# The four compute engines' slots 16 to 79 and SP's layers 1 to 4 of both transformer stacks: unrolled code becomes a loop

## The chip, the cores and the metric

One core of a Trainium2 chip runs the whole program in one launch. The metric is the device time of the program in microseconds; lower is better. A core has five engines, each with its own instruction stream: TensorE (PE), VectorE (DVE), ScalarE (ACT), GpSimd (POOL) and SyncE (SP, which here issues all DMA copies inside the stacks). They meet only through semaphores.

## The reference

A hybrid block over x of 4 sequences x 512 tokens x 128 (float32), four parts, each on the layer norm of x and added to x:

```python
x = x + _L0_attn_a_ref(_layernorm(x), ...)   # retention
x = x + _L0_ffn_ref(_layernorm(x), ...)      # stack 0: six layers
x = x + _L0_attn_b_ref(_layernorm(x), ...)   # a scan over time
x = x + _L0_ffn_ref(_layernorm(x), ...)      # stack 1: the same six layers again
```

The change touches only the two calls of the stack, which is:

```python
def attn_layer(x, Wqkv, qs, ksc, Wo):        # 16 heads of 64, window 32
    q, k, v = split(x @ Wqkv)
    q = l2norm(q) * qs;  k = l2norm(k) * ksc
    q = q * cos * scale + rotate_half(q) * sin * scale
    k = k * cos / scale + rotate_half(k) * sin / scale
    # each window of 32 queries sees its own 32 keys and the 32 before, masked
    return softmax(q @ k.T * 8) @ v @ Wo
def ffn_layer(x, g, bln, W1, b1, W2, b2):
    a, gate = split((layernorm(x) * g + bln) @ W1 + b1)
    return a * gelu(gate) @ W2 + b2
for i in range(6):
    x = attn_layer(shift_tokens(x), ...) + x
    x = ffn_layer(shift_tokens(x), ...) + x
```

## The kernel before

`program` (L2448) runs retention, stack 0, the mixer (the scan) and stack 1; each phase is a block that all engines enter and leave together. Both stacks come out of `ffn_stack` (L348).

**Tiles, groups, slots.** A tile is 128 tokens; a group is the 4 tiles of one sequence in one layer; a stack has 6 layers x 4 sequences = 24 groups = 96 tiles (`TILES`). The work is a software pipeline written out by hand. In slot N an engine works on parts of several tiles at once: the projections of tile N-4, the turning (transposes) of tile N-5 or N-6, the scores of N-6, the softmax of N-7 and N-8, the weighing of the values of N-9, the output projection of N-10, and the MLP of group G-3 or G-4. What a slot holds, and in which order, depends only on its place in the group, T = N % 4. Each of the four compute engines has its own `slot(N, T, G, at, of)` with that order as four branches (PE L719, ACT L985, DVE L1210, POOL L1370). `at(lag)` gives the tile that lies `lag` slots back, `of(lag)` its group. There are 112 slots per stack: 96 and 16 to fill and drain the pipeline; `live` and `live_group` drop the parts of tiles that don't exist.

**`slots` and `run_slots`** (L476, L480) call the slot's body. `run_slots(tile, group, layer, odd, slots_run)` writes `slots_run` slots from tile number `tile` on. In the kernel before there is one call, `run_slots(0, 0, 0, 0, TILES + 16)`, with plain integers: all 112 slots stand in each engine's stream as straight code, with every semaphore value, tile row and address a constant.

**Order between engines.** Every finished step increments a semaphore of its own (`done[...]`); `wait` (L445) and `wait_group` (L451) compare it with tile or group number plus a constant. Beside the data's own waits PE has many that only set its order (L720 to L860). Each engine's instructions run in the order written. Eight PSUM banks: four work banks handed round by the table `BANK`, two for scores (`bank_s`), two for the weighed values (`bank_o`).

**`apart`** (L464) adds 1 to a semaphore that nobody reads, `passed`, and only where the number that it is given is not a plain int. In the kernel before it thus emits nothing. It stands behind the waits of `scores` (L618), `weigh` (L635), the first projection of a group (L602), `mask_max` (L1114), and behind each of SP's waits in `spread_values`, `spread_probs` and `layer_loads`.

**PE** makes each fp32 product as two matmuls with two weight loads in the trace: a projection (`project`, L597) is 128x512, `scores` (L618) is 128 matmuls of 64x64 per tile with no wait inside, `weigh` (L635) 128 of 64x32.

**DVE** does, per tile, four rotations of two instructions (`rotate`, L1065, L1077 and L1079, which read the tables `rot[:, g.layer, T]`), four sums of squares (L1088), the four small steps of the inverse norm (`norms`, L1091), two masks with row maximum (`mask_max`, L1114, 8 pairs of a custom instruction and a read of its accumulator each), two sums and reciprocals, two transposes of the probabilities (L1148), and the residual (`mid`). **ACT** squares, copies out of PSUM and exponentiates; **POOL** adds the rotated halves (L1334), scales them (L1344), and subtracts the maximum and scales in the softmax (L1352, L1360).

**SP** (L495) issues, for each tile, four copies that spread the values to other partitions (`spread_values`, L510) and eight for the probabilities (`spread_probs`, L526), each set behind three waits, and in the first eight tiles of a layer two pieces of the next layer's `w_qkv`, at tile 4 `w_o`, at tile 11 the MLP's weights (`layer_loads`, L544). Weights are double-buffered by layer (`half`). `layer_loads` is called with layer 0, 1, 2, 3, 4, 5 as plain integers.

The code is in none of its parts a loop on the chip.

## Time and profile before

| | us |
|---|---|
| median of 3 runs | 3611.79 |
| lowest, highest | 3595.09, 3617.66 |
| profiled execution, device time | 3617.66 |
| profiled execution, span from first to last instruction | 3615.8 |
| mean granted clock of PE, share of full | 0.967 |
| stack 0, first projection to last weighing | 105.8 to 1607 |
| mixer | about 1640 to 2060 |
| stack 1, first projection to last weighing | 2074.3 to 3580 |

The profile is of one execution. Its page lists each engine's busy time, its slices, the DMA queues, and groups of instructions. "Idle before" is an engine's idle time ahead of an instruction, with what ended it; "issue" there is idle time that ended through nothing the profile shows. PEld is PE's weight load, which overlaps PE. DMA-issuing instructions of SP are listed under SPq. Ends of matmuls are modelled. The queues named "instruction" carry the engines' own code.

### The profile page before, as it was taken

The numbers are of one execution on the slowest core, as the hardware profiler recorded it, in microseconds if no ns is written. First come the engines' busy times: TensorE is split into PE (matmuls) and PEld (weight loads), VectorE is DVE, ScalarE is ACT, GpSimd is POOL, SyncE is SP. The second block draws the span as 40 slices with busy tenths as digits, with TensorE's granted clock in tenths as the row PEclk, the third lists the DMA queues.
The fourth block names the chain that finished last, engine by engine and source line by source line (L and its number), as shares of the span: only waits on it lengthen the run. The fifth ranks groups of instructions, "written<-read, shape, count | busy, mean of one in ns | idle before, by whom it ended". The sixth has DMA issues, their size and how long they took to land. (4 is left out here: it accounts for less than half of the span.)

```text
span 3615.8 us, 151302 instructions
## 1 busy us (share of the span) xinstructions
PE 3373.0 (93%) x60144; PEld 2187.3 (60%) x60144; DVE 3356.0 (93%) x11899; ACT 2045.9 (57%) x3659; POOL 2704.3 (75%) x2440
## 2 busy tenths in 40 slices
PE   6799999999999999988699689999999999999997
PEld 4366666666666666653466446666666666666664
DVE  6899999999999999965799799999999999999994
ACT  2456666665665666654422146666666566666663
POOL 1788888888888888843144288888888888888882
PEclk9899999999999999998799689999999999999999
DMA  1233333333333333320000123333333333333322
GB/s 44 60 88 82 76 91 75 91 78 81 92 76 77 87 81 71 73 66 17 0 1 1 36 49 90 79 89 80 72 93 80 78 90 79 76 92 72 75 67 66
DMA packets 151806, 250.42 MB, mean 69 GB/s; under 512 B 42688, under 2 KB 73408, under 8 KB 150976
## 3 DMA queue, kind: packets, MB, share of 16 engines
q1 hardware_dynamic: 151104, 240.75, 27.8%
q8 instruction: 479, 7.85, 1.0%
q14 instruction: 223, 1.83, 0.2%
HBM read 38.21 MB, written 1.05 MB: 11 GB/s over the span
## 5 line engine op out<-in xcount | busy, mean ns | idle before, releaser
L605 PE MATMUL stack_work<-stack_w_qkv,stack_xst 128*128 128x512 f32 x2304 | 1171.2, 615 | 20.0 <-ACT stack_sq L878 15.6
L1334 POOL TENSOR_TENSOR stack_roped<-stack_rot_c,stack_rot_s 128x512 f32<-128x512 f32 x768 | 973.4, 1280 | 231.7 <-DVE stack_rot_s L1079 120.6
L1344 POOL TENSOR_TENSOR stack_roped<-stack_roped,stack_rnorm 128x512 f32<-128x512 f32 x768 | 790.6, 1043 | 173.3 <-DVE stack_rnorm L1111 173.3
L878 ACT ACTIVATE stack_sq<-stack_work 128x512 f32<-128x512 f32 x768 | 457.2, 595 | 739.7 <-DVE stack_rot_s L1079 734.6
L605 PEld LDWEIGHTS stack_work<-stack_w_qkv,stack_xst 128*128 128x128 f32 x2304 | 388.0, 193 | 289.9 <-issue 219.4
L1077 DVE TENSOR_TENSOR stack_rot_c<-stack_work,rot_tables 128x512 f32<-128x512 f32 x768 | 516.2, 672 | 30.6 <-PE stack_work L605 26.9
L1079 DVE TENSOR_TENSOR stack_rot_s<-stack_work,rot_tables 128x512 f32<-128x512 f32 x768 | 518.7, 675 | 0.0
L1088 DVE TENSOR_REDUCE stack_ssq<-stack_sq 128x8 f32<-128x512 f32 x768 | 512.1, 672 | 3.3
L1122 DVE CUSTOM_DVE_ANT_0 stack_s_m<-stack_bank_s,band 128x64 f32<-128x64 f32 x3072 | 468.9, 215 | 17.7 <-PE stack_bank_s L629 12.8
L614 PEld LDWEIGHTS stack_work<-ident,stack_roped 128*128 128x128 f32 x3072 | 353.6, 141 | 168.9 <-issue 143.2
L614 PE MATMUL stack_work<-ident,stack_roped 128*128 128x128 f32 x3072 | 436.8, 278 | 19.8 <-ACT stack_sq L878 9.8
L1360 POOL TENSOR_TENSOR stack_s_m<-stack_s_m,stack_inv 128x512 f32<-128x512 f32 x384 | 417.0, 1086 | 32.1 <-DVE stack_inv L1140 32.1
L1352 POOL TENSOR_TENSOR stack_s_m<-stack_s_m,stack_smax 128x512 f32<-128x512 f32 x384 | 400.8, 1044 | 32.6 <-DVE stack_smax L1122 30.4
L652 PEld LDWEIGHTS stack_bank_o<-stack_p_pairs,stack_v_even 64*64 64x64 f32 x12288 | 330.0, 135 | 155.5 <-issue 155.3
L665 PEld LDWEIGHTS stack_work<-stack_o_t,stack_w_o 128*128 128x128 f32 x3072 | 364.1, 192 | 80.9 <-issue 58.6
L629 PEld LDWEIGHTS stack_bank_s<-stack_k_t,stack_q_t 64*32 64x32 f32 x24576 | 277.7, 105 | 189.5 <-issue 181.5
L652 PE MATMUL stack_bank_o<-stack_p_pairs,stack_v_even 64*64 64x32 f32 x12288 | 379.0, 221 | 10.3 <-issue 7.3
L652 PE MATMUL stack_bank_o<-stack_p_pairs,stack_v_nat 64*64 64x32 f32 x12288 | 376.7, 219 | 8.1 <-issue 8.0
L665 PE MATMUL stack_work<-stack_o_t,stack_w_o 128*128 128x128 f32 x3072 | 369.4, 276 | 5.0 <-issue 4.0
L629 PE MATMUL stack_bank_s<-stack_k_t,stack_q_t 64*32 64x64 f32 x24576 | 319.3, 225 | 32.8 <-issue 32.5
L652 PEld LDWEIGHTS stack_bank_o<-stack_p_pairs,stack_v_nat 64*64 64x64 f32 x12288 | 331.9, 135 | 9.9 <-issue 9.8
L904 ACT COPY stack_q_t<-stack_work 128x512 f32<-128x512 f32 x384 | 226.5, 590 | 157.5 <-PE stack_work L614 156.9
(255 smaller groups left out, 5110.6 us busy)
## 6 DMA issues: line engine op xcount, KB each, us to landing
stack_v_even<-stack_v_nat SPq DMA_DIRECT2D x768, 128.0 KB, 2.4
stack_p_pairs<-stack_p_turned SPq DMA_DIRECT2D x1536, 64.0 KB
stack_w_qkv<-table_ffn_qkv SPq DMA_DIRECT2D x192, 96.0 KB, 2.2
stack_w_o<-table_ffn_wo SPq DMA_DIRECT2D x12, 512.0 KB, 4.4
stack_w<-table_ffn_w SPq DMA_DIRECT2D x12, 384.0 KB
stack_w<-table_ffn_w SPq DMA_DIRECT2D x12, 192.0 KB
x_outer<-L_attn_a_X SPq DMA_DIRECT2D x4, 256.0 KB, 7.6
ret_xpos<-table_xpos SPq DMA_DIRECT2D x1, 1024.0 KB, 6.9
```

The source lines that it names most:

```text
L605: pe.matmul(work[(BANK["p_" + c][T] + g.row) % 4][:, :], xst[:, g.row, P * T:P * (T + 1)], w_qkv[:, g.half, col:col + 512], start=True, st ...
L614: last = pe.transpose(bank[:, P * n:P * (n + 1)], roped[:, CHUNKS.index(c), T % 2, P * n:P * (n + 1)], ident[:, :])
L629: last = pe.matmul(bank_s[j][WINDOW * n:WINDOW * (n + 1), 64 * hp:64 * hp + 64], q_t[rows, T % 2, hp, WINDOW * n:WINDOW * (n + 1)], k_t[ro ...
L652: last = pe.matmul(bank_o[HD * odd:HD * (odd + 1), two, at:at + WINDOW], values[:, 2 * m + j, :], p_pairs[rows, T % 2, odd_window, j, 2 * ...
L665: last = pe.matmul(bank[:, 0:P], w_o[:, g.half, n, :], o_t[:, T % 2, n, :], start=n == 0, stop=n == PAIRS - 1)
L878: act.activation(sq[:, i % 2, :], work[(BANK["p_" + c][T] + g.row) % 4][:, :], ACT.Square).then_inc(done["squared_" + c], 1)
L1077: dve.tensor_tensor(rot_c[:, i % 2, :].rearrange("p (h d) -> p h d", h=8), src.rearrange("p (h d) -> p h d", h=8), cosine, ALU.mult)
L1079: dve.tensor_tensor(rot_s[:, i % 2, :].rearrange("p (h f d) -> p h f d", h=8, f=2), src.rearrange("p (h f d) -> p h f d", h=8, f=2)[:, :, ...
L1088: dve.tensor_reduce(ssq[:, T % 2, i, :], sq[:, i % 2, :].rearrange("p (h d) -> p h d", h=8), AX.X, ALU.add).then_inc(done["summed_" + c], 1)
L1122: last = dve.tensor_tensor_reduce(s_m[:, T % 2, j, hp, :], bank_s[j][:, 64 * hp:64 * hp + 64], mask[:, first:first + 2 * WINDOW], 1.0, LOW ...
L1334: pool.tensor_tensor(roped[:, i, T % 2, :], rot_c[:, i % 2, :], rot_s[:, i % 2, :], ALU.add).then_inc(done["roped_" + c], 1)
L1344: pool.tensor_tensor(r, r, rnorm[:, T % 2, i, :].unsqueeze(2).broadcast_to([P, 8, HD]), ALU.mult).then_inc(done["united_" + c], 1)
```

## The change

Each compute engine's 112 slots are now emitted in three pieces: slots 0 to 15 as straight code; a loop `Fori(0, 2)` whose body holds 32 slots and runs twice, for slots 16 to 79; and slots 80 to 111 as straight code. The body covers two layers (32 tiles), so that the buffer halves stay constants (`odd` is 1), as do T, the bank, the rows of `xst`, `roped`, `q_t` and so on. Tile, group and layer numbers in it are a register times a constant plus a number; so each semaphore value in `wait`, `wait_group`, `wait_x` and the DMA waits is one, and so is the address `rot[:, g.layer, T]` in DVE's rotations. `live` is always true there, and `apart` emits its increment.

On SP `layer_loads` for layers 1 to 4 becomes one body in `Fori(1, 5)`. Its weight loads have addresses that depend on the layer's register (`w["qkv"][layer]`, and `layer % 2` for the half); the copies of values and probabilities keep constant addresses, and all its waits compare with register values, each followed by `apart`'s increment. Layers 0 and 5 stay straight.

No engine's work, order or buffer is changed. `Fori` is a loop on one engine alone: it adds to a register at the end of the body and branches back while the register is below the end; engines don't meet at it.

```diff
-            run_slots(0, 0, 0, 0, TILES + 16)
+            run_slots(0, 0, 0, 0, 16)
+            with eng.Fori(0, 2) as pair:
+                run_slots(32 * pair + 16, 8 * pair + 4, 2 * pair + 1, 1, 32)
+            run_slots(16 * (DEPTH - 1), 4 * (DEPTH - 1), DEPTH - 1, 1, 16 + 16)
@@ SP
-            for layer in range(1, DEPTH - 1):
+            with sp.Fori(1, DEPTH - 1) as layer:
                 layer_loads(layer, False, False)
```

## Rows read from the trace of the kernel before

**Rows 1.** The page: busy time of the engines, VectorE's 40 slices, an instruction queue
```profile
PE 3373.0 (93%) x60144; PEld 2187.3 (60%) x60144; DVE 3356.0 (93%) x11899; ACT 2045.9 (57%) x3659; POOL 2704.3 (75%) x2440
...
DVE  6899999999999999965799799999999999999994
...
q8 instruction: 479, 7.85, 1.0%
```

**Rows 2.** Windows: us, busy us of each engine (xinstructions), granted clock, DMA share, GB/s
```profile
300.00:600.00 300.00, 297.26 (x5970) 196.09 (x5969) 297.09 (x1142) 191.85 (x346) 259.19 (x237) 1.00 0.35 83
...
900.00:1200.00 300.00, 293.84 (x5823) 193.33 (x5821) 293.35 (x1119) 189.53 (x341) 255.45 (x233) 0.99 0.35 82
```

**Rows 3.** ScalarE's copy of the heads, L929, 150 to 600 us: ns min/median/max, starts
```profile
L929 ACT COPY stack_o_t<-stack_bank_o x29: 1017/1037/1072, 172.8 to 598.7; 128x1024 f32<-128x1024 f32 x29
```

**Rows 4.** Groups by line, 600 to 1100 us: xcount, busy us, mean ns, idle before, releasers
```profile
L1079 DVE TENSOR_TENSOR stack_rot_s<-stack_work,rot_tables 128x512 f32<-128x512 f32 x129 | 87.2, 676 | 0.0
L1077 DVE TENSOR_TENSOR stack_rot_c<-stack_work,rot_tables 128x512 f32<-128x512 f32 x129 | 86.8, 673 | 4.2 <-PE stack_work L605 3.5
...
L605 PEld LDWEIGHTS stack_work<-stack_w_qkv,stack_xst 128*128 128x128 f32 x385 | 64.6, 192 | 42.9 <-issue 33.2 <-ACT stack_sq L878 7.2
```

**Rows 5.** Timeline of TensorE near 861 us: start, us, line, xcount, idle before
```profile
860.64 1.32 PE L629 MATMUL stack_bank_s<-stack_k_t,stack_q_t 64*32 64x64 f32 x107
863.79 0.64 PE L629 MATMUL stack_bank_s<-stack_k_t,stack_q_t 64*32 64x64 f32 x21 [1.82 <-issue]
```

**Rows 6.** The window of 2 us behind that pause, columns as in rows 2
```profile
865.00:867.00 2.00, 2.00 (x3) 0.67 (x2) 1.32 (x11) 0.61 (x2) 2.00 (x3) 0.50 0.91 203
```

**Rows 7.** Timeline of VectorE behind that pause
```profile
869.54 0.59 DVE L1159 TENSOR_TENSOR stack_mshift<-stack_work,stack_xst 64x128 f32<-64x128 f32 x2 [3.22 <-PE stack_work L665]
```

**Rows 8.** Timeline: the first and the last engine to begin one slot
```profile
699.66 0.59 PE L605 MATMUL stack_work<-stack_w_qkv,stack_xst 128*128 128x512 f32 x1
...
701.85 1.28 POOL L1334 TENSOR_TENSOR stack_roped<-stack_rot_c,stack_rot_s 128x512 f32<-128x512 f32 x1 [0.23 <-DVE stack_rot_s L1079]
```

**Rows 9.** Timeline of VectorE, 703 to 715 us
```profile
703.03 0.68 DVE L1079 TENSOR_TENSOR stack_rot_s<-stack_work,rot_tables 128x512 f32<-128x512 f32 x1
...
703.63 0.70 DVE L1148 STREAM_TRANSPOSE stack_p_turned<-stack_s_m 128x512 f32<-128x512 f32 x1
...
709.43 0.21 DVE L1122 CUSTOM_DVE_ANT_0 stack_s_m<-stack_bank_s,band 128x64 f32<-128x64 f32 x1
...
709.57 0.21 DVE L1122 CUSTOM_DVE_ANT_0 stack_s_m<-stack_bank_s,band 128x64 f32<-128x64 f32 x1
...
714.41 0.71 DVE L1148 STREAM_TRANSPOSE stack_p_turned<-stack_s_m 128x512 f32<-128x512 f32 x1 [0.22 <-DMA stack_p_pairs<-stack_p_turned]
```

**Rows 10.** Timeline of SP's queue in the same slot
```profile
710.72 0.59 SPq L541 DMA_DIRECT2D stack_p_pairs<-stack_p_turned  x1
...
711.98 1.53 SPq L498 DMA_DIRECT2D stack_w_qkv<-table_ffn_qkv  x2
713.62 2.42 SPq L522 DMA_DIRECT2D stack_v_even<-stack_v_nat  x4
```

**Rows 11.** Timeline of VectorE behind a run of 16 mask instructions
```profile
872.75 0.18 DVE L1100 TENSOR_SCALAR stack_ssq<-stack_ssq 128x32 f32<-128x32 f32 x1
872.84 0.68 DVE L1077 TENSOR_TENSOR stack_rot_c<-stack_work,rot_tables 128x512 f32<-128x512 f32 x1
```

**Rows 12.** Waits of TensorE in the whole run: us in total, times, longest
```profile
PEld stack_bank_s L629 <- issue: 181.5, 224, 2.0
...
PE stack_bank_s L629 <- issue: 32.5, 32, 1.9
...
PE stack_bank_o L652 <- issue: 15.2, 21, 1.8
```

**Rows 13.** Waits of SP's queue in the whole run
```profile
SPq L535 <- DVE stack_p_turned L1148: 1039.5, 188, 14.4
```

**Rows 14.** VectorE's wait for the probability copies, whole run
```profile
DVE stack_p_turned L1148 <- DMA stack_p_pairs<-stack_p_turned: 2.9, 4, 1.1
```

## The prediction, made before the kernel was run

> **What bounds the kernel now.** I read the page first: TensorE (PE) and VectorE (DVE) are both busy 93% of the span, ScalarE (ACT) 57%, GpSimd (POOL) 75%, and the slices show that the share is lost between the two stacks and at their ends, not inside them [rows 1]. The busy time by stretch confirms it: in 300 us windows inside a stack PE and DVE are each busy 97 to 99% at full granted clock, POOL 86%, ACT 64% [rows 2]. A slot (one tile of 128 tokens passing every engine) takes 15.2 us: the copy of the heads, one per slot, starts 29 times from 172.8 to 598.7 us [rows 3].
>
> Which of the two full engines binds is read from the groups of 500 us. DVE's groups have almost no idle time ahead of them (4.2 us for the first rotation, 0.0 for the second) [rows 4]. PE's weight loads wait for `stack_sq` only 7.2 us in the 500, and for nothing that the profile shows ("issue") 33.2 [rows 4], so PE is nearly full too. I take DVE as the bound with about 1% to spare, and PE as the next one close behind. Anything that keeps either from starting work lengthens the span nearly one for one.
>
> **What the change does to the instruction streams.** The work, its order and its buffers stay. Slots 16 to 79 of each stack (64 of 112, 128 of 224 in all) come out of a loop body of 32 slots that runs twice; SP's layers 1 to 4 come out of a body of one layer that runs four times. Four things are new.
>
> *1. Taken branches.* One per compute engine and stack (slot 47 back to slot 16's code), three per stack on SP. Every body is far longer than what the engine fetches at once: the queue q8 moved 479 packets of instructions, and PE, with 60144 matmuls and as many weight loads, is the one engine with so many [rows 1], some 251 per packet; one body of PE is about 20,000 instructions, DVE's some 2,000 (11899 for 192 tiles). The loop's head is thus not at hand when the engine jumps. The unrolled trace has no taken branch, but it has the price of instructions that aren't there: in the middle of a run of 128 score matmuls, with no wait in the code between them, PE stands still for 1.82 us ended by "issue", and resumes at 863.79, 3.15 us after the run began at 860.64 [rows 5]. I take 3.2 us for a block that must be fetched on demand. That pause cost more than itself: two microseconds later the granted clock is 0.50, the 1.2 GHz level [rows 6], and DVE then idles 3.2 us for PE [rows 7]. So 1.8 us of PE became 3.2 of DVE, 1.4 more. A taken branch: 3.2 + 1.4 = 4.6, say 5 us, if the four engines stall together; they begin a slot within some 2 us of one another (PE's first projection at 699.66, POOL's first sum at 701.85) [rows 8]. Two stacks: 10 us. Bounds: nothing, if the queues cover it and the block is at hand (then 0); 24 us, if the stalls of PE, DVE and POOL follow one another (3 x 3.2 + 1.4 = 11, twice, rounded up).
>
> The Trainium skill, page "Runtime: NRT & Kernel Launch", section "Instruction fetch mechanics", says that a taken branch out of the resident blocks waits for a DMA of the target block, and that kernels therefore prefer to be unrolled; it speaks against this change, and no row of before holds such a branch. "Advanced Engine Details and Errata", section "Control Flow Timing", gives about 108 ns for a compare-and-branch by itself; by that alone the four branches would cost nothing that can be measured, the sum 10 us less.
>
> *2. Waits against a register.* Inside the loop `tile` is a register plus a number, so each of `wait`'s and `wait_group`'s values is one, and has to be formed; so has the table's address in the rotations. By the code DVE's slots have 26 to 54 of them, 40 on average, PE's some 30. No row shows a register value; the nearest show what an instruction costs that the engine only hands out: the mask's pairs start 0.144 us apart, 0.072 us for each of the two, with nothing between them [rows 9], and SP passes three satisfied waits in 0.11 us (the weights end at 713.51, the next issue starts at 713.62) [rows 10]. Where does it show? DVE's instructions of 512 columns start 0.60 us apart whether waits lie between or not (the transpose at 703.63, behind two waits, follows the rotation at 703.03, and leaves no gap) [rows 9]: instructions are handed out ahead, and the cover is 0.6 us per instruction. It is thin only ahead of the short ones: four `norms` steps and two `invert`s in a slot (0.08 to 0.11 us of step), and the two mask runs' first instructions, eight places. Low bound: 0, all hidden. High bound: 0.072 us at all eight places of 128 slots, 74 us. I take one place per slot, the low end, since the short `TENSOR_SCALAR` at 872.75 starts right behind 16 mask instructions and the next rotation 0.09 us later, both with waits ahead of them and no gap [rows 11]: 128 x 0.072 = 9 us.
>
> *3. `apart` becomes real.* It adds a semaphore increment where `n` is no int: two per slot on DVE (mask), four on PE (scores twice, weigh twice), six on SP. On PE they stand ahead of runs for which it can't load weights early anyway: 181.5 us in 224 cases at L629, 0.8 us each, while the matmuls ahead still run (PE itself lacks work there in 32 cases only) [rows 12]. Four steps at DVE's 0.072 are 0.29 us, below 0.8: no charge; without that cover, 128 x 0.29 = 37 us on PE.
>
> *4. SP.* Only the weight loads get register addresses; the 12 copies per tile keep fixed ones. SP's queue has time: it waits 1039.5 us in 188 cases for `p_turned`, 5.5 us each [rows 13]. It is late at one place: in a group's first slot the last of eight probability copies is issued at 710.72, and DVE's next transpose at 714.41 has waited 0.22 us for their landing [rows 9, 10]. Three register waits and three increments at 0.072 are 0.43 us ahead of them. In the whole run DVE waited there 2.9 us in 4 cases [rows 14], so most groups have the slack, and I charge nothing. SP's back edge falls between the copies of a layer's last tile and the wait for the next probabilities, where 3.2 us of fetch fit into the 5.5 that it waits anyway: hidden. What is queued behind it (`v_even` for the next tile) is needed two slots later. Without the cover: 3 x 2 x 3.2 = 19 us.
>
> **Nothing is taken away** that a row charges: the same instructions are fetched and run. The sum against the profiled execution's own time: 3617.7 + 10 + 9 = 3636.7. That execution is the slowest of the three and 5.9 above the median of 3611.8, so 3631 against the median.
>
> **Rivals.**
> *A, the loop is free.* The queues hide branches and registers: 3612. For it: the even 0.60 us step. Against: the pause of 1.82 us shows that a missing block is not hidden. Chance 0.15.
> *B, registers are dear.* All eight short places pay 0.072 us: 74 instead of 9, so 3631 + 65 = 3696; it decides from about 0.2 us per slot on (128 x 0.2 = 26 us, with the branches 36). For it: DVE has 1% spare and 40 waits per slot. Against: no gap in [rows 11]. Chance 0.25, from 3648 to 3733 (with the 37 us of PE too).
> *C, faster.* PE's pauses in wait-free runs (32.5 us in 32 cases at L629, 15.2 in 21 at L652 [rows 12]) depend on where a block ends in a run; the inserted instructions move those ends. At best all go, and DVE, idle 1 us in 100 inside the stacks in the best window [rows 2], wins some 28 of its 2900 us there: 3612 - 28 + 10 = 3594, under 1%. They may as well grow. Chance 0.07.
> *D, SP late in the first slots.* If its six steps cost twice 0.43, 0.4 us would be missing in each of 32 groups: 13 us, 3644. Chance 0.08.
> My forecast has 0.45, from 3618 to 3648.
>
> **How the numbers follow.** Forecast 3631. The range leaves out C's lower half and B's top: 3604 to 3696. A change under 1% (36 us) is about what a measurement of this kernel can't tell from none. Slower by over 1% is B's 0.25 and half of D's: 0.29. Faster by over 1% needs more than I can work out for C; I leave it 0.03 of C's 0.07. The rest, 0.45 + 0.15 + 0.04 + 0.04, is 0.68.
>
> **What would show it.** Step 1: on every compute engine one pause of 3 to 4 us at the end of slot 47 of each stack (slot 9's heads leave at 172.8, so 39 slots of 15.2 later: near 765 us in the first), PE's clock lower behind it, and nothing like it elsewhere. Step 2: the slot inside the loop 15.3 us against 15.2, DVE's 512-column step still 0.60; B shows as gaps or longer steps at `norms`, `invert` and the mask. Step 3: PE's own "issue" waits at L629 and L652 stay near 48 us. Step 4: DVE's wait for `stack_p_pairs` still a few us. I am wrong if the slots outside the loop differ from those inside by more than 0.2 us, if the branch costs much more than 5 us, or if the fetches that follow it come late too.

## The result, and the profile of the changed kernel

The changed kernel takes 3644.3 us (median of 4 runs, 3642.8 to 3651.2) where the kernel before takes 3606.9 us on the same chip (3595.1 to 3617.7). The ratio is 1.0108, with a 95% interval from 1.0072 to 1.0145: slower by about 39 us. The forecast was 3631 us with a range from 3604 to 3696. The profiled execution has a span of 3646.4 us, and stands 2 to 4 us from its median; that of before (3617.7 us) was 11 us above its own.

Lines of the changed file are 3 higher than before (L605 is L608, L629 is L632, L652 is L655, L1077 is L1080). The page first, to be read beside [rows 1]: busy time of the engines, and two instruction queues (packets, MB, share).

```profile
PE 3373.7 (93%) x60144; PEld 2186.3 (60%) x60144; DVE 3341.6 (92%) x11899; ACT 2049.2 (56%) x3659; POOL 2706.3 (74%) x2440
...
q8 instruction: 484, 7.93, 1.0%
q14 instruction: 263, 2.15, 0.2%
```

TensorE's busy time is that of before to 0.7 us, so nothing it does takes longer; what grew is the time in which it does nothing. The waits of the whole run (us in total, times, longest) say where, beside [rows 12]:

```profile
PEld stack_bank_s L632 <- issue: 200.1, 237, 2.1
...
PE stack_bank_s L632 <- issue: 47.6, 45, 2.0
...
PE stack_bank_o L655 <- issue: 25.2, 29, 1.9
```

TensorE's standstills for which the profile shows no cause, all in score and weigh runs, are 72.8 us instead of 47.7. VectorE feels them as waits for TensorE. The groups by line of the whole run, beside the 4.2 us of [rows 4] for 500 us, and SP's waits beside [rows 13]:

```profile
L1080 DVE TENSOR_TENSOR stack_rot_c<-stack_work,rot_tables 128x512 f32<-128x512 f32 x768 | 517.0, 673 | 56.5 <-PE stack_work L608 52.0
```
```profile
SPq L467 <- DVE stack_p_turned L1151: 707.4, 174, 12.8
SPq L538 <- DVE stack_p_turned L1151: 327.0, 60, 13.3
```

The rotation waits 56.5 us where the same group of before has 30.6. SP's queue still waits 1034 us for the probabilities, against 1039.5: it has as much time as before. Last the two places at which the loops turn, in TensorE's timeline (start, us, line, count, idle before) and VectorE's:

```profile
768.66 1.96 PE L608 MATMUL stack_work<-stack_w_qkv,stack_xst 128*128 128x512 f32 x2 [2.97 <-DMA stack_w_qkv<-table_ffn_qkv]
...
770.89 0.69 DVE L1080 TENSOR_TENSOR stack_rot_c<-stack_work,rot_tables 128x512 f32<-128x512 f32 x1 [4.28 <-PE stack_work L608]
```
```profile
2755.57 2.07 PE L608 MATMUL stack_work<-stack_w_qkv,stack_xst 128*128 128x512 f32 x2 [2.61 <-DMA stack_w_qkv<-table_ffn_qkv]
```

The weights named as releaser are long in SBUF there; the profile names the last of several waits. The records of the loop's own instructions show what it is (the loop's line, 760 to 772 us; ns min/median/max, starts): TensorE's branch itself lasts 3.7 us where the same branch, not taken at the loop's end, lasts 0.083, and VectorE's lasts 0.07, but its next instruction stands 3.1 us behind it.

```profile
L491 PEldq COMPARE_BRANCH  x1: 3723/3723/3723, 764.4 to 764.4; - x1
...
L491 DVEq COMPARE_BRANCH  x1: 74/74/74, 766.0 to 766.0; - x1
...
L491 DVEq FUSED_REGOPS  x1: 63/63/63, 769.1 to 769.1; - x1
```

Behind the first of them the granted clock is 0.50, the 1.2 GHz level (windows, columns as in [rows 2]):

```profile
769.00:771.00 2.00, 2.00 (x3) 0.71 (x3) 0.11 (x1) 0.00 (x0) 0.00 (x0) 0.50 0.80 168
```

From the starts of the heads' copy, the group of four slots with the loop's end takes 66.5 us in the first stack and 67.1 in the second, against 61.2 and 60.8 in before: 5.3 and 6.3 us. That is 12 of the 39 us. The other part is in neither one place nor one stack: it is the 25 us of pauses more, spread over 45 + 29 places where before had 32 + 21.

### The profile page after: what moved, and what is told of

It reads as the page before. It is cut to its first block and busy times, and to the rows that moved or that the text cites. A ratio compares the mean times of both kernels' runs of the same rounds, so it can differ in the third digit from the quotient of the medians.

```text
span 3646.4 us, 153624 instructions
## 1 busy us (share of the span) xinstructions
PE 3373.7 (93%) x60144; PEld 2186.3 (60%) x60144; DVE 3341.6 (92%) x11899; ACT 2049.2 (56%) x3659; POOL 2706.3 (74%) x2440
## 5 line engine op out<-in xcount | busy, mean ns | idle before, releaser
L608 PE MATMUL stack_work<-stack_w_qkv,stack_xst 128*128 128x512 f32 x2304 | 1173.6, 615 | 26.9 <-ACT stack_sq L881 16.7
L1080 DVE TENSOR_TENSOR stack_rot_c<-stack_work,rot_tables 128x512 f32<-128x512 f32 x768 | 517.0, 673 | 56.5 <-PE stack_work L608 52.0
L608 PEld LDWEIGHTS stack_work<-stack_w_qkv,stack_xst 128*128 128x128 f32 x2304 | 387.3, 193 | 300.5 <-issue 226.5
L655 PEld LDWEIGHTS stack_bank_o<-stack_p_pairs,stack_v_even 64*64 64x64 f32 x12288 | 330.0, 134 | 155.8 <-issue 155.6
L632 PEld LDWEIGHTS stack_bank_s<-stack_k_t,stack_q_t 64*32 64x32 f32 x24576 | 276.6, 105 | 206.2 <-issue 200.1
L655 PE MATMUL stack_bank_o<-stack_p_pairs,stack_v_nat 64*64 64x32 f32 x12288 | 378.2, 219 | 16.6 <-issue 16.5
L655 PE MATMUL stack_bank_o<-stack_p_pairs,stack_v_even 64*64 64x32 f32 x12288 | 378.8, 220 | 12.4 <-issue 8.8
L632 PE MATMUL stack_bank_s<-stack_k_t,stack_q_t 64*32 64x64 f32 x24576 | 318.5, 225 | 48.0 <-issue 47.6
L655 PEld LDWEIGHTS stack_bank_o<-stack_p_pairs,stack_v_nat 64*64 64x64 f32 x12288 | 333.4, 135 | 20.2 <-issue 20.1
```

Of the source, the lines that this page charges most:

```text
L608: pe.matmul(work[(BANK["p_" + c][T] + g.row) % 4][:, :], xst[:, g.row, P * T:P * (T + 1)], w_qkv[:, g.half, col:col + 512], start=True, st ...
L632: last = pe.matmul(bank_s[j][WINDOW * n:WINDOW * (n + 1), 64 * hp:64 * hp + 64], q_t[rows, T % 2, hp, WINDOW * n:WINDOW * (n + 1)], k_t[ro ...
L655: last = pe.matmul(bank_o[HD * odd:HD * (odd + 1), two, at:at + WINDOW], values[:, 2 * m + j, :], p_pairs[rows, T % 2, odd_window, j, 2 * ...
L1080: dve.tensor_tensor(rot_c[:, i % 2, :].rearrange("p (h d) -> p h d", h=8), src.rearrange("p (h d) -> p h d", h=8), cosine, ALU.mult)
```

## Where the pauses sit

Each pause of before and after can be laid on TensorE's instruction stream, by counting the instructions of the program (a matmul here is four: two passes, each a weight load and a multiplication). Worked out in this way, every pause inside a run is at the end of a block of 256 instructions, in before, in the changed kernel and in the kernels below (in the one with the announced branch after a shift of 15 places in the second stack, which the count doesn't explain). A run of 128 multiplications with their loads is itself 256 instructions, so each of the 384 runs holds one such end. In before, all pauses are at ends that lie 170 or more instructions behind the run's start. In 141 runs the end lies more than 158 behind; 46 of these pause for over 0.2 us, and of the other 243 none.

The queue q8 carries TensorE's blocks, one packet of 16 KB each, and the trace has each packet's start and duration. In the two stacks of before the packet for the next block starts 0.95 us (median) after TensorE enters a block, takes 1.2 us, and in 46 of 46 pauses TensorE resumes 1.15 to 1.66 us (mean 1.39) after the packet's end. The pause of [rows 5] is one: the block before was entered at 856.87, the packet ran from 860.79 to 862.32, and TensorE resumed at 863.79. So a pause is a fetch that comes too late for 256 quick instructions; and it comes late mostly because the packet starts late. In before 74 of 423 packets start over 2 us after the block was entered, in after 94 of 430. The copies are not what holds them: with TensorE in a new block since 258.4 us of before and no copy under way, the packet starts at 262.49. What the late packets follow is in the records of TensorE's sequencer (the part that hands its instructions out; waits that stand as instructions of their own are carried out there): a packet that starts later than 0.6 us ahead of a run starts 1.0 to 1.8 us (median 1.14, 44 cases) after the last such instruction ahead of the run has ended.

The Trainium skill, page "Runtime: NRT & Kernel Launch", section "Instruction fetch mechanics", has the blocks of 256 instructions, the fetch of the next block while one is executed, and says that this is hidden because instructions are handed out more slowly than they are fetched. The blocks agree with the trace; that it is hidden doesn't, for these runs: 256 instructions leave TensorE in 1.5 us, and the packet with what follows it takes 2.6.

## Experiments

The question was which part of the change makes 25 us more of these pauses, and what the rest is. Lines in the experiments are shifted by a few each. The first four split the change.

**TensorE's loop alone** (`if eng.engine == PE: loop, else: run_slots(0, 0, 0, 0, TILES + 16)`, SP straight):

> Only TensorE runs the loop; the other three compute engines and SP keep the straight code of before. Theory P (the loss sits on TensorE: its own pauses inside the score and weigh runs, 47.7 us before and 72.8 us after, plus one stall per back edge): nearly the whole loss is here, 3630 to 3642 us, TensorE's issue waits on bank_s and bank_o together at 66 to 78 us, one pause of 2.5 to 3.5 us at slot 47 of each stack. Theory R (register waits on VectorE, GpSimd and ScalarE): under a quarter of the loss, 3607 to 3617 us. Theory B (all engines' back edges together, 5 to 6 us a stack, and nothing else): 3612 to 3620 us.

3642.0 us, ratio 1.0092 (1.0066 to 1.0119). Pauses of 75.3 us:

```profile
PE stack_bank_s L635 <- issue: 52.0, 50, 1.7
PE stack_bank_o L658 <- issue: 23.3, 29, 1.8
```

**All but TensorE in the loop** (the condition turned round, SP's loop kept):

> TensorE keeps the straight code of before, all other engines and SP run their loops. Theory P: TensorE's issue waits on bank_s and bank_o stay at 45 to 51 us, and only the back edges of the others are left, 4 to 12 us in all: 3611 to 3620 us. Theory R: most of the loss is here, 3630 to 3645 us. If the stalls of the engines at the back edge overlap as forecast, this kernel and the one with TensorE's loop alone each show the whole 5 us a stack at slot 47, so their losses add up to more than that of the changed kernel.

3630.3 us, ratio 1.0040 (1.0021 to 1.0060): 14 us, at the upper edge of theory P and above it by the pauses, 56.5 us where 45 to 51 were expected. VectorE's own stall at the loop's end, with TensorE's work there in time:

```profile
769.00 0.69 DVE L1083 TENSOR_TENSOR stack_rot_c<-stack_work,rot_tables 128x512 f32<-128x512 f32 x1 [3.27 <-issue]
```

The groups with the loop's end are 66.2 and 64.0 us long here, so the other engines alone already show most of a back edge; with TensorE's loop alone they are 65.7 and 67.0, with all loops 66.5 and 67.1: the stalls of the engines at the back edge lie over one another, as forecast. (The two losses, 33 and 14 us, add up to 8 more than the change's 39, which is within their intervals.) The pauses say one thing more: TensorE's stream here is before's, block ends and all, and they are still 9 us longer. So a difference of that size needs no change on TensorE.

**Registers and increments, but no taken branch:**

```diff
-            with eng.Fori(0, 2) as pair:
-                run_slots(32 * pair + 16, ...)
+            for first in range(2):
+                nc.regs_mov(held, first)
+                pair = nc.snap(held, min_val=0, max_val=1)
+                run_slots(32 * pair + 16, ...)
```

> The loop body is written out twice with the pair's number held in a register (and SP's layers four times), so every register wait, every register address and every increment of apart is there and no engine takes a branch back. Theory B (the branches cost 5 to 6 us a stack): 10 to 12 us less than the changed kernel, 3630 to 3636 us if the rest of the loss stays. Theory P with block ends alone: TensorE's issue waits in the runs follow where the 256-instruction blocks end; by the pauses seen at each such place in the two traces so far they come to some 54 us here, so 3607 to 3622 us. Theory I (the increments and register instructions themselves make each block end dearer, wherever it falls): 66 to 78 us of issue waits as in the changed kernel, and 3630 to 3636 us.

3645.8 us, ratio 1.0103 (1.0060 to 1.0145), pauses of 75.2 us. So the pauses don't need a branch, and they don't follow from the place of the block ends alone (54 us by that). The groups at slot 47 are 62.2 and 62.8 us long: the 5 to 6 us of the back edge are gone there. In the time of the whole kernel 10 us can't be told with these intervals.

**The kernel before with the increments of `apart`, constant waits, no loop** (the condition `if not isinstance(n, int)` taken out):

> The kernel before with one edit: apart always adds its increment, in all slots (six per slot on SP, four on TensorE, two on VectorE), with constant waits and no loop. Theory I: TensorE's issue waits on bank_s and bank_o grow from 47.7 to 65 us or more (over all 192 slots, not 128 of them), time 3620 to 3640 us. Theory P with block ends alone: by where the block ends now fall, some 50 us, the time 3602 to 3614 us.

3652.2 us, ratio 1.0104 (1.0063 to 1.0145): the increments alone, with none of the change's loops, registers or branches, cost as much as the change, in all slots instead of two thirds of them.

```profile
PE stack_bank_s L628 <- issue: 57.7, 46, 2.6
PE stack_bank_o L651 <- issue: 22.7, 27, 2.2
```

80.4 us of pauses. This fells theory P with place alone (some 50 us expected). It doesn't say whose increments.

**Increments on TensorE alone** (`if eng.engine == PE: eng.sem_inc(passed, 1)`):

> The kernel before, with apart's increment added on TensorE alone (constant waits, no loop). Theory I (an increment ahead of a run makes TensorE ask for its next block of instructions later): the whole loss of the kernel with increments on all engines comes back, 3640 to 3656 us, with 70 to 85 us of TensorE's issue waits on bank_s and bank_o, and the packets of the instruction queue start later ahead of the score run of a group's last slot (at its first matmul instead of 1.3 us before). Theory S (the increments on SP or VectorE do it, by moving the copies): no more than half of the loss, under 3630 us, and 45 to 60 us of issue waits. Theory P (only where the 256-instruction blocks end): as much as before, 3605 to 3615 us, about 50 us of issue waits.

3645.1 us, ratio 1.0094 (1.0068 to 1.0121), pauses of 75.1 us. It is TensorE's four increments per slot; SP's six and VectorE's two add nothing that can be told.

**A constant wait in the place of each** (`eng.wait_ge(consts_set, N_CONSTS * (run + 1))`):

> As the one with TensorE's increments alone, but each increment is replaced by one more wait, on a semaphore that reached its value long ago: the extra step stays, nothing is incremented. Theory I in its narrow form (it must be an increment, which has to wait for the matmuls ahead of it): back to 3605 to 3618 us and 45 to 58 us of issue waits. Theory W (any instruction of its own between the last wait and the first matmul does it): 3635 to 3656 us and 68 us or more.

3619.6 us, ratio 1.0021 (1.0005 to 1.0037), 57.8 us of pauses. One more wait at each place costs 8 us (2 to 13 by the interval), the increments 34 (25 to 44).

How do the increments do that? Not by holding up the run: in the kernel with increments everywhere, in the changed one and in before, the first weight load of a run starts 0.51 to 0.57 us behind the start of the multiplication ahead of it, on average over each of the eight kinds of run (scores and weighing, four slots of a group). Compare one run of scores of a group's last tile, slot T = 1 (the expectations call it the score run of a group's last slot), with the block's end 190 and 191 instructions behind its start, in before and in the kernel with TensorE's increments (timelines of TensorE):

```profile
2446.40 1.88 PE L605 MATMUL stack_work<-stack_w_qkv,stack_xst 128*128 128x512 f32 x4
2448.21 1.88 PE L629 MATMUL stack_bank_s<-stack_k_t,stack_q_t 64*32 64x64 f32 x128
```
```profile
1048.99 1.88 PE L605 MATMUL stack_work<-stack_w_qkv,stack_xst 128*128 128x512 f32 x4
1050.80 1.15 PE L629 MATMUL stack_bank_s<-stack_k_t,stack_q_t 64*32 64x64 f32 x94
1053.53 0.51 PE L629 MATMUL stack_bank_s<-stack_k_t,stack_q_t 64*32 64x64 f32 x34 [1.57 <-issue]
```

The same two projections (four multiplications) lead to the run. In before the packet starts at 2446.86, 1.35 us ahead of the run, and ends at 2448.38, and the run goes through with a hitch of 0.12 us. With the increment it starts at 1050.73, as the run begins, ends at 1052.23, and TensorE stands until 1053.53. Over all runs of that kind whose block ends more than 165 behind the start, worked out from the packets' starts:

```
                                      cases   packet later than 0.6 us
                                              ahead of the run
before                                 17        2
before + constant wait on TensorE      24        2
others loop                            17        4
TensorE's registers alone              19       11
TensorE's increments alone             17       12
increments everywhere                  17       14
registers, increments, no branch       18       10
loop, constant wait, no increments     15       12
loop, constant wait, announced         14        7
TensorE's loop alone                   17        8
changed kernel                         17        8
```

The other seven kinds differ less. Of the 24 us that the changed kernel's pauses are longer, this kind has 10 (3.4 to 13.2 us); with TensorE's increments alone it has 13 (3.4 to 16.5), and the weigh runs of slot T = 3 have 7 (2.4 to 9.1). The score runs of slot T = 3 are late in before too, 16 of 16, and have 18 us of its pauses; those of T = 0 are late once in 16 in before and twice in 16 with an increment ahead of each.

The traces have the reason, and it is not the increment by itself. The last thing that such a run waits for is VectorE's mask (`masked0`, seen 1.17 us ahead of the run in both cases above). In before that wait rides on the run's first weight load, and the sequencer's last instruction of its own starts at 2445.8, 2.4 us ahead of the run:

```profile
L449 PEldq EVENT_SEMAPHORE  x2: 51/51/51, 2445.7 to 2445.8; - x2
```

An increment is an instruction of the sequencer's own, and the wait for the mask has gone into it (3526 weight loads carry a wait in before, 2950 here). It can't be passed before the mask is there, and starts at 1049.7, 1.1 us ahead of the run:

```profile
L467 PEldq EVENT_SEMAPHORE  x1: 51/51/51, 1049.7 to 1049.7; - x1
```

In both the packet starts 1.0 us after that instruction has ended. The constant wait left the mask's on the weight load (3526 again), so its packets are as early as before's. And in the changed kernel's loop all ten runs of the table carry the increment: in the six with block ends at 214 to 241 the mask comes 1.17 us ahead of the run, the instruction ends 1.09 ahead and the packet starts 0.05 to 0.19 behind the run's start, 1.4 us later than in before; in the four at 183 or 184 the mask was there earlier, the instruction ended 2.13 to 2.38 ahead, and the packets came 0.98 to 1.38 ahead, with a short pause or none. No run here moves the wait alone, without an increment; this is read from the traces.

**The loop without TensorE's increments.** A wait on a constant now stands first in each group of waits, and the run's first weight load takes that one:

```diff
+        def known(n, *values):
+            if not isinstance(n, int):
+                for value in values:
+                    nc.tensor.lower_val(value)
+                nc.tensor.wait_ge(consts_set, N_CONSTS * (run + 1))
-                apart(pe, t)          # scores, weigh, project
```

> The changed kernel with TensorE's increments taken out: a wait on a constant that was reached long ago stands first in each group of waits, so that no matmul of a run carries a wait against a register and apart isn't needed on TensorE. Loops, register waits and the other engines' increments stay. Theory I (TensorE's increments are the larger part of the loss, about 30 us of 38): what is left is the back edges (10 to 12 us) and the extra step (up to 7), a ratio to before of 1.002 to 1.005, that is 3617 to 3630 us, and 45 to 60 us of issue waits on bank_s and bank_o. Theory R (register arithmetic or the loop on TensorE does the same without increments): a ratio of 1.008 or more and 68 us or more of issue waits.

3635.2 us beside 3603.1, ratio 1.0103 (1.0085 to 1.0121). A miss: I expected 1.002 to 1.005. The pauses are down to 59.2 us (45.2 and 14.0), inside the expected band, the time is not. The table above has the reason for a part: all ten packets in slots 16 to 79 are late (12 of 15 in all), though nothing is incremented. Register arithmetic is left there, and, since the weight load has the constant's wait, the mask's wait is again an instruction of its own. Ahead of the ten late ones the sequencer stands in it for 1.0 to 1.5 us, till the mask is there; here the one ahead of the run of 854.47:

```profile
L449 PEldq EVENT_SEMAPHORE  x2: 51/580/1110, 852.1 to 852.2; - x2
```

TensorE's part of this was tried by itself.

**Register waits on TensorE alone**, written out twice as above, with the constant wait and no increments, all else as before:

> TensorE alone has register waits and register arithmetic in slots 16 to 79, written out twice with no loop and no branch, and with no increments (the constant wait stands first, as in the kernel with that edit). Everything else is the kernel before. Theory R (register instructions ahead of a run hold back the fetch of the next block as an increment does): a ratio to before of 1.005 to 1.010, 62 us or more of TensorE's issue waits on bank_s and bank_o, and the instruction packets ahead of the score run of a group's last slot start at the run's first matmul in the register part. Theory I (only increments do, and the loss left in the loop without them is branches and the other engines): a ratio under 1.004 and 47 to 58 us of issue waits.

3628.8 us beside 3605.5, ratio 1.0063 (1.0042 to 1.0083), 23 us, and 61.5 us of pauses, half a microsecond short of the expected 62. The packet ahead of the last slot's score run starts within 0.1 us of the run in 8 of 12 cases among slots 16 to 79, and in none of the 7 outside. These 23 us are not the price of register arithmetic by itself: the constant wait is in them, and the mask's wait stands alone here too (the sequencer stands in it for 1.3 us ahead of each of the nine late runs of the register part). No run has the registers with that wait on the weight load. The increments and this edit delay the packets of the same runs, so their prices (34 and 23 us) can't be added.

**The back edge announced** (the same, `hint_back_edge=True` on each engine's loop):

> The same, and in addition every engine's loop says at the top of its body where its closing branch will go, so that the head can be fetched before the branch is taken. If the 5 to 6 us a stack at slot 47 are the wait for the head's block: 8 to 12 us less than without the hint, and no pause over 0.6 us on TensorE between slots 47 and 48. If the hint is lost long before the branch (the body is some 20,000 TensorE instructions long) or the stall is of another kind: the same time within 3 us and the same pause of 2.5 to 3 us.

3632.0 us, ratio 1.0082 (1.0065 to 1.0098) where the kernel without the hint has 1.0103 in the same comparison: 7.6 us by the ratios, 3.3 by the medians, with intervals that overlap. The traces are clearer: the groups with the loop's end take 62.3 and 63.6 us, with the hint, 66.5 and 67.0 without it. In the first stack the stall is gone: TensorE's taken branch lasts 0.50 us instead of 3.6. In the second it lasts 3.6 still, so the announcement did nothing for TensorE there, and why stays open; one pause is left, 2.9 us long, but the clock's loss behind it is shorter:

```profile
2747.41 1.12 PE L613 MATMUL stack_work<-stack_w_qkv,stack_xst 128*128 128x512 f32 x2 [2.94 <-DMA stack_w_qkv<-table_ffn_qkv]
```

**Block ends moved on purpose.** Two kernels pad TensorE's straight stream of before with empty instructions ahead of two weigh runs per group: `pe.addr_align(256, offset=95 and 101, max_nops=255)`, and the same with offset 2.

> The kernel before, with TensorE's stream padded at two places of each group (ahead of the weigh runs of slots 1 and 3, some 70 empty instructions a group) so that the end of a 256-instruction block falls 16 to 158 instructions behind the start of every score and weigh run. In the four traces with positions worked out, a pause needs a block end more than 158 instructions behind the start of the run. Theory F (pauses are late fetches of the next block, and place decides): the issue waits of TensorE inside the runs fall from 47.7 to under 8 us and the time falls by a third to two thirds of the 45 us that go, 3575 to 3598 us. Theory N (pauses come from contention whose place in time is fixed, and only move): 35 us or more of issue waits stay, 3600 to 3615 us. If the padding costs on the path, up to 48 x 70 x 5.6 ns = 19 us come on top.

> The same padding with other offsets: the first instructions of the weigh runs of slots 1 and 3 stand near the start of a block, so that the block ends fall some 250 and 230 behind the starts of the weigh and score runs of slot 1, and 250 and 200 behind those of slot 3. Theory F: about 3.5 us of pauses in each of 48 groups, 120 to 190 us of issue waits inside the runs, and 3670 to 3760 us. Theory N: 35 to 60 us of issue waits and 3600 to 3630 us.

3911.0 us (ratio 1.0826) and 4092.5 us (1.1334). Both times are far from what was expected, because an empty instruction costs far more than 5.6 ns: they start 0.071 us apart in the trace. One of a group's two paddings, 51 instructions, shows as 2.23 us of standstill, and in the slots with little work at each stack's end paddings of up to 255 show as up to 18 us. The place, though, does what theory F says. With early ends the waits of the whole run have no more line for TensorE at the score runs; the groups by line show

```profile
L629 PE MATMUL stack_bank_s<-stack_k_t,stack_q_t 64*32 64x64 f32 x24576 | 310.3, 225 | 0.2
```

0.2 us of idle time against 32.8 in before, and in slots 48 to 79 of each stack TensorE's whole idle time is 17.9 us, eight times the padding's 2.23. With late ends there are 150 standstills at the weigh runs (54 with early ends) and 20 at the score runs:

```profile
PE stack_bank_o L652 <- issue: 246.7, 150, 11.9
...
PE stack_bank_s L629 <- issue: 13.1, 20, 1.9
```

Between the two lie 181 us. The padding is nearly the same in the full slots (71 and 76 instructions a group); at the stacks' ends the second kernel has more, and all its 669 more would be 48 us at 0.071 each.

**Runs cut in two**, with no padding, straight stream, no increments: what followed a run now stands between its halves, for all eight runs of a group:

```diff
                     scores(*at(6), 0)
-                    scores(*at(6), 1)
                     wait(pe, "v_out0", N - 7)
                     project(*at(6), "v0")
+                    scores(*at(6), 1)
```

> The kernel before with no loop and no increments, but each of TensorE's score and weigh runs is cut in two: the projection, transposes or gate matmul that followed the run now stand between its halves (0.4 to 1.3 us of other work), with the waits that stood ahead of it. Theory F (a pause is the time by which the next block's packet comes too late for a run of 256 quick instructions): the issue waits on bank_s and bank_o fall from 47.7 to 5 to 20 us, and the time by 12 to 30 us, 3580 to 3598 us. Rival: the operations moved ahead by half a run find their inputs or banks not ready, and TensorE waits for ACT, VectorE or a bank what it saved: 3600 to 3630 us.

3677.4 us, ratio 1.0209 (1.0191 to 1.0227): slower by 75 us, and mostly not by the rival's reason. The pauses do go, 8.2 us instead of 47.7:

```profile
PE stack_bank_o L652 <- issue: 4.5, 7, 1.3
PE stack_bank_s L629 <- issue: 3.7, 7, 1.3
```

But each run that begins costs its own lead, and there are twice as many. The page, and the weight loads' waits at the starts (for bank_s beside [rows 12]; for bank_o before has 165.1 us in 215 cases):

```profile
PE 3472.7 (94%) x60144; PEld 2177.1 (59%) x60144; DVE 3352.2 (91%) x11899; ACT 2051.3 (56%) x3659; POOL 2709.7 (74%) x2440
```
```profile
PEld stack_bank_o L652 <- issue: 239.4, 385, 1.6
PEld stack_bank_s L629 <- issue: 231.8, 340, 1.5
```

TensorE counts as busy for 100 us more: 384 more changes into a run at 0.26 us each. VectorE waits 73.6 us for scores (12.8 in before); TensorE's waits for ACT ahead of transposes, the rival's reason, grow by 10 us (9.8 to 20.0). No kernel of this study is faster than before.

All together, worked out from the matmuls' starts and ends: pauses inside runs, TensorE's idle time in all slots of both stacks, and the ratio.

```
                                     pauses  us    idle us   ratio to before
before                                 49   47.1   118.8
before + constant wait on TensorE      56   57.2   126.4     1.0021
others loop                            58   55.5   135.6     1.0040
TensorE's registers alone              66   61.4   141.0     1.0063
loop, constant wait, announced         57   55.9   141.3     1.0082
TensorE's loop alone                   77   74.9   155.3     1.0092
TensorE's increments alone             73   75.0   150.9     1.0094
loop, constant wait, no increments     63   58.3   141.8     1.0103
registers, increments, no branch       75   74.8   150.6     1.0103
increments everywhere                  72   80.1   159.6     1.0104
changed kernel                         72   72.6   151.5     1.0108
```

For eight of the ten kernels that were changed, idle time more than before and time lost agree within 7 us (32.7 and 39 for the changed kernel, 32.1 and 34 for TensorE's increments, 22.2 and 23 for its registers). For the two loops with the constant wait it is 23 against 37 and 22 against 30. The profiled execution of before is 11 us above its median, which makes before's idle time look large, but that would shift all rows alike. The 8 to 14 us between stay open: no run here says whether they are pauses of other executions or something else.

## Why the prediction was right, and which of its steps were not

The time lies in the range, and 13 us above the point. On the chip that ran both, the loss was 37 us by the medians where the forecast's sum has 19. The ratio lies at the very edge of the 1%: the interval, 0.7 to 1.5%, holds both the case that the text gave 0.68 and the one that it gave 0.29.

*Step 1, taken branches: right.* 10 us forecast, 5.3 + 6.3 seen in the two groups; TensorE's branch is at 764.4, where 765 was named, and its work resumes at 768.66. TensorE stands 2.97 and 2.61 us (3.2 was taken from a late block of before), VectorE 4.28, 1.3 more, with the clock at half behind the stall, for which the sum had 1.4. The engines stall together: either half of the loops has most of the stall. Without a branch the groups are 62.2 and 62.8 us long. In the time of the whole kernel the branches can't be told: the kernel without them has 1.0103, this one 1.0108. The sentence on the Trainium skill's page "Runtime: NRT & Kernel Launch", by which a taken branch out of the resident blocks waits for its target, agrees; by the 108 ns of "Advanced Engine Details and Errata", section "Control Flow Timing", these two places would not exist; the trace has some 0.08 us on TensorE for a branch that is not taken, and 3.7 for the taken ones.

*Step 2, register waits: the size near, the place wrong.* 9 us were charged to VectorE's short instructions. They cost nothing there: inside the loop a short step and the rotation or product behind it, both with register waits, still start 0.08 us apart:

```profile
773.26 0.17 DVE L1103 TENSOR_SCALAR stack_ssq<-stack_ssq 128x32 f32<-128x32 f32 x1
773.34 0.75 DVE L1180 SCALAR_TENSOR_TENSOR stack_hid<-stack_work,stack_vec,stack_hid 128x512 f32<-128x512 f32 x1
```

and the kernel with all loops but TensorE's loses 14 us with both back edges in it. The count was wrong too: the text took 40 values to be formed in a slot of VectorE and 30 in one of TensorE, and the trace of the changed kernel has 494 and 404 register instructions on them, 3.9 and 3.2 per looped slot. On TensorE's side the kernel with its register waits loses 23 us, in which the moved wait for the mask and the constant wait are contained. The text asked for VectorE's cover only, because it took VectorE as the bound, and gave TensorE's 30 register waits no sum of their own. "Both are full" should have meant that TensorE gets its own sum.

*Step 3, `apart` becomes real: this is the step that failed.* "Four steps at VectorE's 0.072 are 0.29 us, below 0.8: no charge", and TensorE's pauses would stay near 48 us. The cover was there and did its work: no run begins later. But the sum counted only the start of a run, and the price falls some 170 to 250 instructions later, at the end of a block whose packet starts 1.0 us after the sequencer's last own instruction: with the increment that instruction also waits for the mask, and ends 1.1 us ahead of the run instead of 2.4. The measured price is 34 us alone, near the 37 that the text gave for the case without cover, by another mechanism. The pauses went to 72.8 us, which the text had named as the sign that this step is wrong.

*Step 4, SP: right.* 1034 us of waiting left against 1039.5, VectorE's wait for the copies 2.5 us in 3 cases (2.9 in 4 in [rows 14]), and six increments per slot on SP that cost nothing beside TensorE's.

*The rivals.* A fell with the 5 to 6 us at each back edge. B named registers, but at VectorE's short steps and with 65 us more, neither of which is seen. C had the right object, pauses set by where blocks end, and said they may as well grow. By place alone, taking for each run of the changed kernel the pause of before's runs of the same kind with the nearest block ends, they come to 51 us, where before itself gives 46: place accounts for about 5 of the 25 us, less than the 9 by which the pauses grew with TensorE's stream untouched. D is not seen.

So the total came out near since the back edges were sized right and 9 us charged to the wrong place stood in for some of the 27 that are left of the 39, most of them TensorE's late blocks; that second part is luck, and the range had room for the rest.

## What to carry to other kernels

Ask of each edit on a nearly full TensorE not only whether it delays the next matmul, but where its sequencer stands ahead of a long run of short matmuls: there the next 256 instructions have to be on their way before the run begins. Edits that turned the wait that ends last from a part of the first weight load into an instruction of its own (an increment, or a constant wait that took its place) cost 34 and 23 us here, with no visible gap at the place where they stand. If a long body is looped, leave the engine with the shortest instructions unrolled (1.0040 against 1.0108 here), and look in the trace at which wait its weight loads carry. That keeping the data's wait there is enough, with registers and increments elsewhere, no run here has tried. The announced back edge gained 3 to 8 us, within the noise. And when two engines are full, make a sum for each.

## What the hardware showed that I had not expected

- Every pause of TensorE inside a wait-free run, in before too, is the end of a block of 256 instructions, with resumption 1.15 to 1.66 us after the block's packet has ended. With block ends early in each run the pauses at the score runs go from 32.5 us to 0.2.
- The packet's start is not bound to the entry into a block: 0.95 us after it in the median, up to 4.1 us with the copies' queue empty. The late ones start 1.0 to 1.8 us (median 1.14) after TensorE's last wait or increment that is an instruction of its own.
- A satisfied constant wait costs little (8 us for four in each of 192 slots); increments at the same places, with the mask's wait inside them, 34 us.
- TensorE's branch lasts 3.7 us when taken and 0.083 when not; announced, 0.50 in one stack and 3.6 in the other.
- An empty instruction on TensorE takes 0.07 us, as long as some 12 instructions of a score run.
- Cutting 384 runs of short matmuls in two costs 0.26 us of TensorE's time per cut, more than the 0.12 us per run that the pauses cost on average.
